# Summing attention probabilities on GpSimd: one running sum for all off-diagonal tiles of a block instead of one sum for every four tiles

## What is computed

```
scores = einsum('bhqd,bhkd->bhqk', q, k) / sqrt(32)      # + causal mask
attn   = softmax(scores, axis=-1)
out    = einsum('bhqk,bhkd->bhqd', attn, v)
```

## Time and profile before

| what | us |
|---|---|
| median of 3 runs | 2930.88 |
| the profiled execution's own time | 2931.07 |
| its span in the trace | 2929.3 |
| TensorE matmul busy | 2871.9 |
| VectorE busy | 1814.1 |
| GpSimd busy | 1066.9 |
| ScalarE busy | 1051.6 |

### The profile page before, as it was taken

How to read it: one execution, slowest core, us unless ns; L and a number is a source line. 1 busy time by engine, 2 the same in 40 slices (tenths; PEclk the granted TensorE clock), 3 DMA queues, 4 the chain that set the end, 5 groups by cost and what they waited for, 6 DMA issues and landing times. The chain is left out here.

```text
span 2929.3 us, 49495 instructions
## 1 busy us (share of the span) xinstructions
PE 2871.9 (98%) x19280; PEld 2334.2 (80%) x19280; DVE 1814.1 (62%) x3321; ACT 1051.6 (36%) x1827; POOL 1066.9 (36%) x745
## 2 busy tenths in 40 slices
PE   7999999999999999999999999899999999999999
PEld 5888888888888877877777777678888888888887
DVE  5656565556565645477777775665656555666664
ACT  4322222222222223256666664432222222222222
POOL 3322222222222214566677763332222222222221
PEclk9999999999999999999999999999999999999999
DMA  3000000000000004842233231100000000000001
GB/s 101 29 22 29 22 28 22 21 21 26 25 25 25 8 18 91 238 110 61 61 75 72 60 96 54 43 23 29 22 29 21 29 21 21 21 29 21 29 8 58
DMA packets 98630, 127.86 MB, mean 44 GB/s; under 512 B 43068, under 2 KB 51244, under 8 KB 95148
## 3 DMA queue, kind: packets, MB, share of 16 engines
q1 hardware_dynamic: 98476, 125.72, 15.3%
HBM read 96.34 MB, written 29.34 MB: 43 GB/s over the span
## 5 line engine op out<-in xcount | busy, mean ns | idle before, releaser
L59 PE MATMUL psum<-ffn_x_high,ffn_w_high 128*128 128x512 f32 x2048 | 800.1, 391 | 16.7 <-DVE ffn_gelu L466 14.8
L60 PE MATMUL psum<-ffn_x_low,ffn_w_high 128*128 128x512 f32 x2048 | 797.9, 390 | 0.0
L61 PE MATMUL psum<-ffn_x_high,ffn_w_low 128*128 128x512 f32 x2048 | 797.8, 390 | 0.0
L612 POOL TENSOR_TENSOR ffn_inner<-ffn_gelu,ffn_inner 128x512 fp32r<-128x512 f32 x256 | 346.2, 1352 | 1156.5 <-ACT ffn_inner L549 1156.5
L456 DVE SCALAR_TENSOR_TENSOR ffn_gelu<-ffn_gelu,psum 128x512 f32<-128x512 f32 x256 | 176.1, 688 | 606.7 <-ACT ffn_gelu L542 606.7
L59 PEld LDWEIGHTS psum<-ffn_x_high,ffn_w_high 128*128 128x128 f32 x2048 | 385.2, 188 | 100.4 <-DVE ffn_gelu L466 17.8
L61 PEld LDWEIGHTS psum<-ffn_x_high,ffn_w_low 128*128 128x128 f32 x2048 | 385.1, 188 | 80.3
L60 PEld LDWEIGHTS psum<-ffn_x_low,ffn_w_high 128*128 128x128 f32 x2048 | 385.3, 188 | 79.5
L59 PE MATMUL psum<-ffn_inner,ffn_w_high 128*128 128x512 f32 x1024 | 398.6, 389 | 0.2
L60 PE MATMUL psum<-ffn_inner,ffn_w_high 128*128 128x512 f32 x1024 | 398.4, 389 | 0.0
L61 PE MATMUL psum<-ffn_inner,ffn_w_low 128*128 128x512 f32 x1024 | 398.4, 389 | 0.0
(11 more groups left out here) (123 smaller groups left out, 3592.7 us busy)
## 6 DMA issues: line engine op xcount, KB each, us to landing
ffn_words<-packed SPq DMA_DIRECT2D x96, 256.0 KB
ffn_word_scales<-scales SPq DMA_DIRECT2D x96, 256.0 KB
qk_parts<-parts SPq DMA_DIRECT2D x32, 512.0 KB, 3.9
queries<-qk_parts SPq DMA_DIRECT2D x48, 256.0 KB, 4.1
keys<-qk_parts SPq DMA_DIRECT2D x48, 256.0 KB, 6.6
v_parts<-parts SPq DMA_DIRECT2D x16, 256.0 KB, 3.0
values<-v_parts SPq DMA_DIRECT2D x16, 256.0 KB, 7.8
out<-x SPq DMA_DIRECT2D x16, 256.0 KB, 2.0
```

What stands on the lines that cost most here:

```text
L59: pe.matmul(out, w_high, x_high, start=first, stop=False, skip_group_check=True)
L60: pe.matmul(out, w_high, x_low, start=False, stop=False, skip_group_check=True)
L61: return pe.matmul(out, w_low, x_high, start=False, stop=last, skip_group_check=True)
L612: pool.tensor_tensor(inner[:, tb % 2, m, 1, :], product[m], f32(inner[:, tb % 2, m, 0, :]), ALU.subtract)\
```

## The change

GpSimd makes one running sum per block: of the 12 tiles of batches 0, 1, 2 (11 adds), of the 8 tiles of batches 4, 5 (7 adds), and of the 4 tiles of batch 7 (3 adds). That is 21 adds a head where there were 18. TensorE meets each of the three sums with the ones once, inside the block's diagonal batch (3, 6, 8), ahead of its last round. That is 3 rounds a head where there were 6. The constants of the waits follow.

```diff
-QUADS = [i for i in range(BATCHES) if BATCH * i not in DIAGONAL_TILES]
+TOTALS = [(0, 1, 2), (4, 5), (7,)]
+TOTAL_MET_IN = {total[-1] + 1: c for c, total in enumerate(TOTALS)}
+ADDS_DONE = dict(zip([i for total in TOTALS for i in total],
+                     itertools.accumulate(BATCH - (i == total[0]) for total in TOTALS for i in total)))
+ADDS = max(ADDS_DONE.values())
...
-            def meet_quad(hp, s, i):
-                c = QUADS.index(i)
-                pe.wait_ge(quad_steps, 54 * hp + 18 * (s + 1) + 3 * (c + 1))
+            def meet_total(hp, s, c):
+                pe.wait_ge(quad_steps, 3 * ADDS * hp + ADDS * (s + 1) + ADDS_DONE[TOTALS[c][-1]])
                 for q in range(QUARTERS):
-                    last = sum_lane(quads[:, c % NQUADS, :], q, 0)
+                    last = sum_lane(quads[:, (len(TOTALS) * s + c) % NQUADS, :], q, 0)
                 last.then_inc(quads_met, 1)
...
-                        if n == BATCH * QUARTERS and i - 1 in QUADS:
-                            meet_quad(hp, s, i - 1)
+                        if n == BATCH * QUARTERS and i in TOTAL_MET_IN:
+                            meet_total(hp, s, TOTAL_MET_IN[i])
...
-                if u % BATCH == 0 and summed and i % BATCHES in QUADS:
-                    act.wait_ge(quad_steps, 54 * hp + 18 * (s + i // BATCHES + 1) + 3 * (QUADS.index(i % BATCHES) + 1))
+                if u % BATCH == 0 and summed and i % BATCHES in ADDS_DONE:
+                    act.wait_ge(quad_steps, 3 * ADDS * hp + ADDS * (s + i // BATCHES + 1) + ADDS_DONE[i % BATCHES])
...
-            def add_quad(hp, s, i):
...
+            def add_up(hp, s, c):
+                total = quads[:, (len(TOTALS) * s + c) % NQUADS, :]
+                t0 = BATCH * TOTALS[c][0]
+                steps = 3 * ADDS * hp + ADDS * (s + 1) + (ADDS_DONE[TOTALS[c - 1][-1]] if c else 0)
+                tiles = [probs[:, (SLOTS * s + t0 + j) % RING, :] for j in range(BATCH * len(TOTALS[c]))]
+                pool.wait_ge(quads_met, 3 * len(TOTALS) * hp + (len(TOTALS) * s + c + 1))
+                pool.wait_ge(probs_ready, 120 * hp + (SLOTS * s + t0 + 2))
                 pool.tensor_tensor(total, tiles[0], tiles[1], ALU.add).then_inc(quad_steps, 1)
-                for j in (2, 3):
+                for j in range(2, len(tiles)):
                     pool.wait_ge(quad_steps, steps + j - 1)
-                    pool.wait_ge(probs_ready, 120 * hp + (SLOTS * s + BATCH * i + j + 1))
+                    pool.wait_ge(probs_ready, 120 * hp + (SLOTS * s + t0 + j + 1))
                     pool.tensor_tensor(total, total, tiles[j], ALU.add).then_inc(quad_steps, 1)
```

More of the change, by code:

```diff
@@ L1 @@
+import itertools
 from contextlib import ExitStack
@@ L1426, in meet_batch @@
                                 last = sum_lane(tiles[j], q, j if diagonal else 0, last_head)
-                if i - 1 in QUADS and not diagonal and not last_head:
-                    meet_quad(hp, s, i - 1)
+                if i in TOTAL_MET_IN and not diagonal and not last_head:
+                    meet_total(hp, s, TOTAL_MET_IN[i])
                 if t0 + BATCH - 1 in OUT_DONE:
@@ L1638, in _ @@
                 pool.memset(start[:, e + 1:e + 2], 0.0).then_inc(out_stored[e], 80)
-            pool.memset(start[:, 5:6], 0.0).then_inc(quad_steps, 18)
+            pool.memset(start[:, 5:6], 0.0).then_inc(quad_steps, ADDS)
             pool.memset(start[:, 6:7], 0.0).then_inc(quads_met, NQUADS)
@@ L1642, in _ @@
                 for s in range(3):
-                    for i in QUADS:
-                        add_quad(hp, s, i)
+                    for c in range(len(TOTALS)):
+                        add_up(hp, s, c)
             pool.wait_ge(o.wo_high_ready, 1)
```

## The result

The changed kernel takes 2939.43 us, the median of 8 runs (2938.35 to 2943.0), against 2930.68 us before (8 runs, 2929.39 to 2931.49): a ratio of 1.0032, 95% interval 1.0022 to 1.0043. It is slower by 8.75 us. The forecast was +10.2.

A forecast was written before the change was run, and what follows sets the result against it. TensorE, busy 98% of the span, was taken to bound the kernel. First head +0.86 us, fourteen heads of +0.68 (+9.5) and -0.22 at the end make +10.2: 2941.2 us, own range 2938 to 2944, 80% range 2934.5 to 2947.

The forecast's parts named there:

- Three rounds less, 0.22 us each: TensorE's rounds of ones for batches 0, 1 and 4 go: 0.66 us a head, 9.9 us in all without waiting.
- The chain of 11 dependent adds: GpSimd's first sum: 11 adds in one chain take 14.94 us, 1.365 us a dependent step; before, 9 adds took 11.96.
- Two free steps become dependent: Inside GpSimd's first sum, two steps of 1.25 us become dependent ones of 1.365, adding 0.25 us to the chain.
- The rival that left this out: Only the number of adds counts, not dependence: chain 14.55 us, head 33.05, +4.4 us, 2935.3 us; chance 0.10.
- The loop: Meet to next head's first add 18.40 us, chain 14.94, way to TensorE 0.10: 33.44 us a head against 32.76 before.
- The way from GpSimd to TensorE: From the end of GpSimd's last add to TensorE's matmul: 0.1 us taken, from a range of 0.05 to 0.15.
- The wait: TensorE waits ahead of the first sum's meet in slot 15: about 1.36 us, given as 1.2 to 1.4.
- The second sum level with its meet: The second sum's 7 adds end 9.44 us behind the first sum, as TensorE reaches that meet; costed at nothing.
- the third rival: The second sum is late too: +0.2 us a head, 3 us in all, 2944.2 us; chance 0.09.
- The clock: Rival: TensorE's wait in each head lowers its clock, 24 us in all, 2965 us, or 2953 in half the heads; chance 0.05.
- the other three: TensorE's saving stands (2921.1 us, chance 0.05), only adds count (2935.3, chance 0.10), second sum late too (2944.2, chance 0.09).
- The sum: Whole kernel: first head +0.86, fourteen heads +9.5, behind the last meet -0.22; in all +10.2 us, 2941.2 us.

The follow-up runs named there:

- block2_only: Kernel before with only batches 4 and 5 sharing a sum, batches 0, 1, 2 keeping one each (19 adds, 5 rounds a head): 2927.73 us, ratio 0.9987.
- split_eight_four: Changed kernel, but batches 0 and 1 share a sum and batch 2 has its own (20 adds, 4 rounds a head): 2924.20 us, ratio 0.9979.
- two_sums: Changed kernel with the same adds and rounds, but GpSimd keeps two running sums by turns and adds them at the end: 2931.66 us, ratio 1.0002.
- rounds_ahead: Changed kernel plus two rounds of ones a head on TensorE, ahead of the wait for the first sum: 2941.03 us, ratio 1.0031.
- rounds_behind: Changed kernel plus two rounds of ones a head on TensorE, in batch 4's meet, behind the first sum's meet: 2946.26 us, ratio 1.0053.
- block3_only: Changed kernel, but batches 4 and 5 get a sum each again, the twelve-tile sum stays (20 adds, 4 rounds a head): 2942.67 us, ratio 1.0040.
- pair_and_two_sums: Changed kernel, but VectorE adds tiles 10 and 11 and GpSimd keeps two running sums by turns (3 rounds a head): 2931.24 us, ratio 1.0006.

## Why the prediction was right, step by step

The mechanism came out as forecast: a chain that is late for its meet, and a loop through TensorE's list that carries the lateness from head to head.

- **Three rounds less, 0.22 us each.** Right: block2_only gives a head of 32.52 for 32.76, split_eight_four 32.31 with two rounds less.
- **The chain of 11 dependent adds.** 14.90 us for 14.94; the dependent step is 1.36 us.
- **Two free steps become dependent.** The rival that left this out had a chain of 14.55 us and a head of 33.05; 14.90 and 33.39 exclude it. two_sums shows it from the other side: with the same 21 adds a head is 0.64 us faster, and would be faster still without its wait for a tile.
- **The loop.** From the meet to the next first add 18.44 us in the mean for 18.40, which offsets the chain's 0.04. rounds_ahead and rounds_behind show that just this part of TensorE's list counts.
- **The way from GpSimd to TensorE.** 0.05 us for 0.10. A head takes 33.39 us for 33.44, which is 14 x 0.05 = 0.7 us of the difference.
- **The wait.** 1.0 us as matmul idle time and 1.3 as idle time of the loads, for 1.36 forecast. I named 1.2 to 1.4 without saying which count. The loads' is the one that fits, and it agrees with the 1.29 us that a head loses against TensorE's list.
- **The second sum level with its meet.** Right, and by a hair: in each of the 15 heads that meet's first weight load starts within 0.01 us of the end of the second sum, and its matmul 0.10 to 0.13 behind that end. The matmul comes 9.47 us behind the first meet in the mean, and TensorE's list alone gave 9.44, so hardly any time is lost. Adds of the second sum slower by 2% would have brought the third rival about; that it stayed away owes something to luck.
- **The clock.** 1.00 from 1279.60 to 1747.05; a wait of this size did not lower it. That rival did not come about, nor the other three.
- **The sum.** +8.75 between medians and +9.6 between profiled executions, for +10.2. What the stage itself shows is +9.6 to the last meet, where the forecast had 10.4: 0.7 from the head's time, 0.1 from the first head. The other parts of the profiled difference, -1.3 ahead of the stage and +1.5 behind it, lie in code outside the change, were not forecast and nearly cancel: that the total came so close is in part luck. The second feed-forward part kept its length; the first came out 1.3 us shorter. The profiled execution after lies 1.3 us above its kernel's median and the one before 0.4 above its own, so the medians differ by 0.9 us less.

The load of GpSimd as a rival of its own was not in the prediction; block3_only and split_eight_four exclude it, one slower and one faster than before with 20 adds each.

## What to carry to other kernels

To join partial sums saves the meets but puts all of their adds in one chain that must be done by the first deadline; compare the chain's length from its first input to its meet with the time that the busiest engine needs for the same stretch, not the engines' busy shares. Once the busiest engine waits in a loop, work ahead of the wait is free up to the wait's length and work behind it counts, so a piece can be given back to it (one tile direct, or one sum more) to shorten the chain: here one round of 0.22 us took 1.36 off the chain and 1.05 off the head. Stop the joining where both lengths are equal.

## What the runs showed of the hardware that was not expected

- An add from SBUF on VectorE beside GpSimd's adds took up to 1652 ns where it takes 684 by itself, and one of GpSimd's adds took 1.61 us instead of 1.29.
- It holds for the smallest operations. VectorE turns the maxima into their two parts by a cast and a subtraction on 128x4 right behind it. The cast takes 170 ns at the least, and waited in the kernel before already: 366 ns in the median, up to 740 beside the adds of the sums and 1202 elsewhere. The subtraction took 162 to 166 ns in all 64 cases before, up to 1199 in the changed kernel, and 1195 in the median in two_sums. VectorE's busy time rose by 30 us (1814.1 to 1843.8) with the same instructions, about half in the casts and half in the subtractions. In the changed kernel this was off the path.
- GpSimd's adds follow each other 1.25 us apart when independent and 1.36 when one waits for the one before. That gap decides whether the subtraction gets in. VectorE, then GpSimd, in the changed kernel:
```profile
1478.79 1.12 DVE L873 CAST max_parts<-minus_max 128x4 fp32r<-128x4 f32 x1
1479.95 1.20 DVE L875 TENSOR_TENSOR max_parts<-minus_max,max_parts 128x4 fp32r<-128x4 f32 x1
...
1489.40 1.18 DVE L873 CAST max_parts<-minus_max 128x4 fp32r<-128x4 f32 x1
1490.61 0.16 DVE L875 TENSOR_TENSOR max_parts<-minus_max,max_parts 128x4 fp32r<-128x4 f32 x1
```
```profile
1478.63 1.26 POOL L1640 TENSOR_TENSOR quads<-quads,probs 128x512 f32<-128x512 f32 x1
1479.85 1.28 POOL L1636 TENSOR_TENSOR quads<-probs 128x512 f32<-128x512 f32 x1
...
1489.26 1.28 POOL L1636 TENSOR_TENSOR quads<-probs 128x512 f32<-128x512 f32 x1
1490.62 1.29 POOL L1640 TENSOR_TENSOR quads<-quads,probs 128x512 f32<-128x512 f32 x1
```
Both casts end as an add of GpSimd ends (1479.89 and 1490.54). The first of these is the end of a sum, the next add is independent and already under way, and the subtraction ends only with it. Behind the second the next add is dependent, and the subtraction is done in 0.16 us. All cases in the traces fall the same way. Where the cast ends with an add that an independent one follows, the subtraction took over 1.1 us in 15 of 15 cases in the changed kernel, 42 of 42 in two_sums and 29 of 29 in pair_and_two_sums. Where a dependent add follows, it was short in all 44 cases before and in all 29 of the changed kernel.
- So a faster GpSimd cost TensorE time: in pair_and_two_sums TensorE waits for these steps. No run changed the gap alone; the cases of one trace, sorted by the step that follows, are the evidence.
